# Attribute stage of a graph network kernel: tail repair of two parts moved into the last batches, and twelve row gathers moved ahead of the stage's end

## What is computed

```python
edge_proj = edge_attr @ W_sum + b_sum
sum3d = jax.ops.segment_sum(edge_proj, src, num_segments=num_nodes)
return x + z_in[in_deg] + z_out[out_deg] + cent_term + vor_term + sum3d
```

## Time and profile before

| | us |
|---|---|
| median of 3 runs | 5778.88 |
| lowest and highest | 5772.54, 5779.97 |
| the profiled execution, its own time | 5781.98 |
| its span in the profile | 5780.3 |
| mean granted TensorE clock | 0.711 of full speed |
| busy: PE (TensorE) / DVE / ACT (ScalarE) / POOL | 3737.6 / 4533.3 / 1445.9 / 3515.7 |

### The profile page before, as it was taken

How to read it: one execution, slowest core, us unless ns; L and a number is a source line. 1 busy time by engine, 2 the same in 40 slices (tenths; PEclk the granted TensorE clock), 3 DMA queues, 4 the chain that set the end, 5 groups by cost and what they waited for, 6 DMA issues and landing times.

```text
span 5780.3 us, 46191 instructions
## 1 busy us (share of the span) xinstructions
PE 3737.6 (65%) x13476; PEld 2458.1 (43%) x13476; DVE 4533.3 (78%) x7871; ACT 1445.9 (25%) x4020; POOL 3515.7 (61%) x3626
## 2 busy tenths in 40 slices
PE   2777777986666626999996444444444444455899
PEld 1655666873444415666664111111112111123566
DVE  8787888989356627888766999999999999997334
ACT  1333333333333313333221111111111111112322
POOL 3777777777777775433313777777777777775000
PEclk8555555555555557999998677777777777777899
DMA  3544444444433332211114888888888888886000
GB/s 87 158 157 149 150 152 152 151 146 153 150 103 102 115 108 59 69 59 63 60 40 144 265 287 277 282 282 276 287 277 282 283 277 288 276 277 193 22 20 26
DMA packets 328279, 968.57 MB, mean 168 GB/s; under 512 B 84476, under 2 KB 124101, under 8 KB 315994
## 3 DMA queue, kind: packets, MB, share of 16 engines
q0 software_dynamic: 198672, 578.35, 32.9%
q1 hardware_dynamic: 80970, 211.35, 10.3%
q10 hardware_dynamic: 48384, 175.92, 7.8%
HBM read 670.63 MB, written 294.73 MB: 167 GB/s over the span
## 4 chain that ended last, share of the span: by engine, by line
PE 42%; POOL 28%; issue 11%; ACT 8%; DVE 7%; DMA 2%; ACTq 2%; SPq 0%; DVEq 0%; POOLq 0%
POOL big L1803 25%; PE bank L909 16%; ACT bank L957 6%; PE bank L1556 5%; PE bank L1545 4%; PE bank L855 4%; PE bank L2482 3%; PE bank L2474 3%; POOL big L596 3%; PE bank L1567 2%; ACT big L932 1%; PE bank L2032 1%; ACTq L942 1%; DMA big<-keys_values,idx 1%; PE bank L2357 1%
## 5 line engine op out<-in xcount | busy, mean ns | idle before, releaser
L1803 POOL DMA_INDIRECT big<-keys_values,idx x1674 | 1591.3, 951 | 510.3 <-issue 507.9
L596 POOL DMA_INDIRECT big<-in_edge_attr,big x1568 | 1524.5, 972 | 609.5 <-issue 459.9
L2032 PE MATMUL bank<-big,ident 128*128 128x512 f32 x1674 | 957.3, 738 | 1155.0 <-DVE big L1883 1119.6
L909 PE MATMUL bank<-big,ident 128*128 128x128 f32 x2976 | 1125.0, 481 | 526.6 <-ACT bank L957 508.2
L2032 PEld LDWEIGHTS bank<-big,ident 128*128 128x128 f32 x1674 | 391.8, 241 | 1719.9 <-DVE big L1883 1226.0
L909 PEld LDWEIGHTS bank<-big,ident 128*128 128x128 f32 x2976 | 737.7, 307 | 835.9 <-ACT bank L957 720.9
L957 ACT ACTIVATE bank<-bank,big 128x128 f32<-128x128 f32 x1485 | 508.0, 342 | 1261.8 <-PE bank L909 1256.5
L1905 DVE TENSOR_TENSOR big<-big,bank 128x1536 f32<-128x1536 f32 x279 | 480.0, 1750 | 123.8 <-DMA big<-keys_values,idx 123.8
L648 DVE TENSOR_TENSOR big<-big,bank 128x1024 bf16<-128x1024 bf16 x400 | 486.1, 1215 | 96.8 <-PE bank L855 96.5
L1910 DVE TENSOR_REDUCE big<-big 128x48 f32<-128x1536 f32 x279 | 486.6, 1745 | 0.0
L1915 DVE TENSOR_TENSOR big<-big,bank 128x1536 f32<-128x1536 f32 x279 | 477.9, 1740 | 0.0
(11 more groups left out here) (360 smaller groups left out, 4605.7 us busy)
## 6 DMA issues: line engine op xcount, KB each, us to landing
running_sums<-big ACTq DMA_DIRECT2D x196, 512.0 KB, 2.8
running_attention<-big SPq DMA_DIRECT2D x46, 1632.0 KB, 7.7
queries_by_row<-big ACTq DMA_DIRECT2D x139, 512.0 KB
big<-queries_by_row SPq DMA_DIRECT2D x46, 1536.0 KB, 8.8
big<-keys_values,idx POOLq DMA_INDIRECT x1674, 3.9
big<-in_edge_attr,big POOLq DMA_INDIRECT x1568
keys_values<-big SPq DMA_DIRECT2D x5, 1792.0 KB, 6.9
big<-x_after_layer SPq DMA_DIRECT2D x7, 896.0 KB, 5.6
```

Source lines behind the costliest of these rows:

```text
L596: pool.indirect_dma_start(out=z.rows[:, r, k, :], out_offset=None, in_=w["edge_attr_128"][:, :], in_offset=bass.IndirectOffsetOnAxis(ap=z. ...
L909: pe.matmul(sum_of(k), lhsT=m.ident[:, :], rhs=z.rows[:, r, k, :], start=False, stop=True, skip_group_check=True).then_inc(s_sum, 1)
L1803: pool.indirect_dma_start(out=kv[:, r, k, :], out_offset=None, in_=t["kv"][:, :], in_offset=bass.IndirectOffsetOnAxis(ap=m.idx2[:, c:c + 1 ...
L2032: mm = pe.matmul(bank[pair % 4][:, :], lhsT=m.ident[:, :], rhs=kv[:, b % RINGK, i * S + j:(i + 1) * S + j + 1:S, D:KW], start=(j == 0), st ...
```

## The change

Nothing is computed differently. POOL's list, DVE's tail work and TensorE's tail products are put in another order:

- the three lookups come before the gathers of batch 190, the two row gathers of parts 0 and 1 before batch 192, the two scatters of these parts (each with its wait for landing) before batch 195;
- DVE does `tail_places` for all parts and the additions of parts 0 and 1 after batch 193; only part 2's addition is left behind the last batch;
- the twelve gathers of chunk 0's sums move from the node stage into the attribute stage (`first_sums`, into a buffer of their own, `f.sg0`): eight after the last batch, four after part 2's scatter; four of the eight degree gathers (`z_out`) are now the last thing in POOL's list of the stage;
- the 129 spare rows of `running_sums` move from its end to its beginning, so that gathers from parts 0 and 1 can be declared to read only the rows below part 2;
- POOL, in the node stage, starts with the gathers of chunk 1, after a wait for the twelve.

```diff
-SUMROWS = PLACES + P + 1
+SPARES = P + 1
+SUMROWS = SPARES + PLACES
...
     def gpsimd(pool):
+        def repair(h, q):
+            pool.indirect_dma_start(out=t["sums"][:, :], out_offset=bass.IndirectOffsetOnAxis(ap=q.to_i, axis=0),
+                                    in_=q.main, in_offset=None).then_inc(s_fixed, 16)
+            pool.wait_ge(s_fixed, 16 * (h + 1))
+
+        def first_sums(h):
+            early = slice(0, SPARES + P * PART_START[NP1 - 1]) if h < NP1 - 1 else slice(0, SUMROWS)
+            for b in range(CHUNKS[0]):
+                pool.indirect_dma_start(out=f.sg0[:, h, b, :], out_offset=None, in_=t["sums"][early, :],
+                                        in_offset=bass.IndirectOffsetOnAxis(ap=m.lastpos[:, h, b:b + 1], axis=0)
+                                        ).then_inc(f.rows, 16)
+
         for b in range(B1):
...
+            if b == B1 - 6:
+                pool.wait_ge(s_tabst, 32 * (NP1 + 1))
+                pool.wait_ge(s_trash, 32)
+                for h, q in enumerate(z.tails):
+                    pool.wait_ge(s_look, h + 1)
+                    pool.indirect_dma_start(out=q.row_i, out_offset=None, in_=t["lastpos"][h][:, :],
+                                            in_offset=bass.IndirectOffsetOnAxis(ap=q.look, axis=0)).then_inc(s_found, 16)
+            if b == B1 - 4:
+                pool.wait_ge(s_found, 16 * NP1)
+                for q in z.tails[0:NP1 - 1]:
+                    pool.indirect_dma_start(out=q.main, out_offset=None, in_=t["sums"][0:SPARES + P * PART_START[NP1 - 1], :],
+                                            in_offset=bass.IndirectOffsetOnAxis(ap=q.row_i, axis=0)).then_inc(s_main, 16)
+            if b == B1 - 1:
+                pool.wait_ge(s_fix, NP1 - 1)
+                for h, q in enumerate(z.tails[0:NP1 - 1]):
+                    repair(h, q)
...
-        gather_degrees(pool, m, w, f, 0, range(2, 2 * CHUNKS[0] - NP1))
+        q = z.tails[NP1 - 1]
+        pool.indirect_dma_start(out=q.main, out_offset=None, in_=t["sums"][:, :],
+                                in_offset=bass.IndirectOffsetOnAxis(ap=q.row_i, axis=0)).then_inc(s_main, 16)
+        gather_degrees(pool, m, w, f, 0, range(2, 4))
         pool.wait_ge(s_fix, NP1)
-        for h, q in enumerate(z.tails):
-            pool.indirect_dma_start(out=t["sums"][:, :], out_offset=bass.IndirectOffsetOnAxis(ap=q.to_i, axis=0),
-                                    in_=q.main, in_offset=None).then_inc(s_fixed, 16)
-            gather_degrees(pool, m, w, f, 0, range(2 * CHUNKS[0] - NP1 + h, 2 * CHUNKS[0] - NP1 + h + 1))
-            pool.wait_ge(s_fixed, 16 * (h + 1))
+        repair(NP1 - 1, q)
+        first_sums(NP1 - 1)
+        gather_degrees(pool, m, w, f, 0, range(4, 2 * n))
...
-        for k in range(1, NP1):
-            ins = v.tensor_scalar(z.table[0:64, k], z.table[0:64, k], float(P * PART_START[k]), None, ALU.add)
+        for k in range(NP1):
+            ins = v.tensor_scalar(z.table[0:64, k], z.table[0:64, k], float(SPARES + P * PART_START[k]), None, ALU.add)
...
-        gather(0, 0, NP1 * CB)
-        pool.wait_ge(s_vr, 1)
+        pool.wait_ge(f.rows, 16 * NP1 * CHUNKS[0])
         gather(1, 0, NP1 * CB)
```

More of the change, by code:

```diff
@@ L464, in gpsimd @@
         st.add(pool.iota(m.pidx[:, :], [[0, 1]], base=0, channel_multiplier=1, allow_small_or_imprecise_dtypes=True))
-        st.add(pool.iota(m.trash1[:, :], [[0, 1]], base=PLACES, channel_multiplier=1,
+        st.add(pool.iota(m.trash1[:, :], [[0, 1]], base=0, channel_multiplier=1,
                          allow_small_or_imprecise_dtypes=True))
@@ L472, in gpsimd @@
         st.add(pool.memset(f.nodes, 0.0))
-        st.add(pool.memset(z.trash[:, 0, :], PLACES + P))
+        st.add(pool.memset(z.trash[:, 0, :], P))
         st.add(pool.memset(z.trash[:, 1, :], ROWS + P))
@@ L744, in shadow @@
         for k in range(NP1):
-            st.add(v.tensor_scalar(m.lastpos[:, k, :], last[:, k, :], float(P * PART_START[k]), None, ALU.add))
+            st.add(v.tensor_scalar(m.lastpos[:, k, :], last[:, k, :], float(SPARES + P * PART_START[k]), None, ALU.add))
         st.add(v.tensor_scalar(m.has[:, :], deg, 1.0, None, ALU.min))
@@ L832, in vector @@
                                        in1=z.rows[:, r, k, :], op0=ALU.mult, op1=ALU.add).then_inc(s_sum, 1)
[L833 to L836, removed]
+            if b == B1 - 3:
+                dve.wait_ge(s_found, 16 * NP1)
+                for q in z.tails:
+                    tail_places(dve, v, st, q, m.trash1[:, :])
+                dve.wait_ge(s_prod, 1)
+                dve.wait_ge(s_main, 16 * (NP1 - 1))
+                for h, q in enumerate(z.tails[0:NP1 - 1]):
+                    v.tensor_tensor(q.main, q.main, bank[7][:, h * P:(h + 1) * P], ALU.add).then_inc(s_fix, 1)
+        dve.wait_ge(s_prod, 2)
         dve.wait_ge(s_main, 16 * NP1)
-        for h, q in enumerate(z.tails):
-            v.tensor_tensor(q.main, q.main, bank[7][:, h * P:(h + 1) * P], ALU.add).then_inc(s_fix, 1)
+        q = z.tails[NP1 - 1]
+        v.tensor_tensor(q.main, q.main, bank[7][:, (NP1 - 1) * P:NP1 * P], ALU.add).then_inc(s_fix, 1)
     def tensor(pe):
@@ L916, in tensor @@
         pe.wait_ge(s_eq, 1)
+        pe.wait_ge(s_saved, NP1 - 1)
+        for h, q in enumerate(z.tails[0:NP1 - 1]):
+            mm = pe.matmul(bank[7][:, h * P:(h + 1) * P], lhsT=q.eq, rhs=z.saved[:, h], start=True, stop=True, skip_group_check=True)
+        mm.then_inc(s_prod, 1)
         pe.wait_ge(s_copied, 2 * B1)
[L918 to L922, removed]
+        pe.matmul(bank[7][:, (NP1 - 1) * P:NP1 * P], lhsT=z.tails[NP1 - 1].eq, rhs=z.rows[:, (B1 - 1) % RING1, GB - 1, :],
+                  start=True, stop=True, skip_group_check=True).then_inc(s_prod, 1)
     def scalar(act):
-        into = [t["sums"][P * at:P * (at + n), :].rearrange("(p k) f -> p k f", p=P) for at, n in zip(PART_START, PART_COLS)]
+        into = [t["sums"][SPARES + P * at:SPARES + P * (at + n), :].rearrange("(p k) f -> p k f", p=P) for at, n in zip(PART_START, PART_COLS)]
         qz = t["qrow"][0:ROWS, :].rearrange("(p k) d -> p (k d)", p=P)
@@ L1033, in node_inputs @@
     f.zout, end = cut(m.big, end, CB, D)
+    f.sg0, end = cut(m.big, 4 * CB * D - NP1 * CHUNKS[0] * FE, NP1, CHUNKS[0], FE)
     f.rows = m.sem("node_rows_gathered")
@@ L1123, in node_stage, with sums_of @@
     RA = RV = 4
+    def sums_of(c):
+        return late_sg if c else f.sg0
     def pairs(c, j):
@@ L1197, in gather @@
                 col = slice(CHUNK_AT[c] + b, CHUNK_AT[c] + b + 1)
-                pool.indirect_dma_start(out=sg[:, h, b, :], out_offset=None, in_=t["sums"][:, :],
+                pool.indirect_dma_start(out=late_sg[:, h, b, :], out_offset=None, in_=t["sums"][:, :],
                                         in_offset=bass.IndirectOffsetOnAxis(ap=m.lastpos[:, h, col], axis=0)
```

21 lines of the change are left out of this document (7 added, 14 removed).

## The result

| | before | after |
|---|---|---|
| median (20 runs each) | 5780.51 | 5791.09 |
| lowest and highest | 5772.54, 5785.66 | 5786.03, 5796.85 |
| the profiled execution, its own time | 5781.98 | 5793.27 |
| its span | 5780.3 | 5791.6 |
| mean granted TensorE clock | 0.711 | 0.724 |

Ratio 1.0018, 95% interval 1.0012 to 1.0025: 10.6 us slower, which is inside the 0.2% that I called no change, and not zero. The predicted time was 5786.2 and the range 5779 to 5795.

The account below looks back on a forecast made before the run. POOL's list of DMA issues was taken to bound the attribute stage's end. `mask_sums` 5.3 us late, plus 1.0 for stretched issues and 1.0 for landing under loads, gave 7.3: 5778.88 + 7.3 = 5786.2 us, range 5779 to 5795.

Parts of the forecast that it names:

- the first rival: Node stage opens only when POOL has issued its whole list: `mask_sums` 13.6 us late, 5792.5 us; chance 0.12.
- POOL paces the last batches, each insert is on the path: Last edge batches: inserted lookups, row gathers and scatters add 11.45 us to POOL's list, none of it hidden.
- Hidden inserts: Rival: something other than POOL paces batches 190 to 195, so 11.45 us go: -4.2, 5774.7 us; chance 0.06.
- DVE's part is hidden: After batch 193: DVE's 8.1 us of tail work fit within POOL's 10.3 before the scatters; spare 2.2 us.
- The stage opens at the landing of the third scatter: Node stage's start: DVE begins when that scatter has landed, at 2174.7, 5.95 us late.
- Degree rows become what DVE waits for: Ahead of `add_terms`: DVE waits 1.7 us for the eighth degree gather; `mask_sums` 5.3 us late.
- Stretch of POOL's issues: Degree gathers early in the node stage: POOL's issue takes longer beside DVE's work; 1.0 us, bounds 0 and 1.7.
- Landing under SP's loads: Last degree gathers land in 3.7 us beside SP's loads, 1.0 more than 2.7; bounds 2.7 and 4.6.
- The clock and late stores: TensorE's clock rise: same pattern expected, rival -10 or as much up, chance 0.07; `running_sums` stores: nothing unless over 20 us more.
- the mechanism's own bound: Upper limit of the forecast's lateness with its terms at their bounds: 5.3 + 1.7 + 1.9 + 0.9 = 9.8 us.

Follow-up runs that it names:

- experiment 3: Changed kernel, but POOL leaves the attribute stage only when all eight degree gathers have landed; 5800.73 us, ratio 1.0032 to the kernel before.
- experiment 5: Changed kernel, but the two scatters stand ahead of the first and fourth edge gather of batch 195; 5787.74 us, ratio 1.0009 to the kernel before.
- Experiment 2: Changed kernel, but the last four degree gathers are issued before the four gathers of part 2's sums; 5785.83 us, ratio 1.0005 to the kernel before.
- experiment 4: Changed kernel, but chunk 0's twelve sum gathers return behind the stage's end, degree gathers ahead of the third scatter; 5787.61 us, ratio 1.0007 to before.
- experiment 6: Experiment 4 joined with experiment 5: sums and degree gathers moved back, scatter waits covered; 5780.25 us, ratio 0.9997 to the kernel before.
- experiment 8: Kernel before, but POOL leaves the stage without awaiting the third scatter's landing; its first sum gather waits instead; 5783.36 us, ratio 1.0001.
- experiment 1: Changed kernel, but SP's loads of bias and input rows also wait for the eight degree gathers' landing; 5791.98 us, ratio 1.0014 to before.
- experiment 7: Experiment 6, but POOL leaves the stage once the third scatter is issued; only part 2's sum gathers await its landing; 5778.08 us, ratio 0.9988 to before.

## Why the prediction was right, and what in it was not

The time fell into the range, but that says little about the mechanism. The range was made wide enough for the first rival too, and by the time alone its 5792.5 fits 5791.09 better than my 5786.2 does. What decides is the stage's start in the timeline and experiment 3.

- **POOL paces the last batches, each insert is on the path.** Right. The loop cost 11.73 us (last edge gather, 80.52 for 68.79); predicted 11.45. One of the three scatters landed in 2.7 us, not 2.3, which is the 0.3 that I had left in the bounds. Hidden inserts (-4.2) are ruled out by this and by experiment 5.
- **DVE's part is hidden.** Right: its two additions were done at 2142.56, and POOL came to the scatters at 2144.64 with its usual 0.30 us. The spare was 2.1 us, predicted 2.2.
- **The stage opens at the landing of the third scatter.** Right: L2556 at 2178.81 is 2.3 us behind 2176.49, with eight gathers still to be issued, and experiment 3 shows the 11.7 us of the alternative. Start 6.25 us late; predicted 5.95.
- **Degree rows become what DVE waits for.** Right in kind. Experiment 2 takes the wait away by order alone.
- **Stretch of POOL's issues, predicted 1.0.** Too much: the issues of 2182.79 to 2188.16 took 1.06, 1.06, 1.03, 1.00 and 0.95, together 0.4 us over 0.95 each. What I had not read is where in DVE's work the long issue of before begins. DVE's row of before beside the 1.96 us at 2174.43:

```profile
2174.35 1.23 DVE L1283 TENSOR_TENSOR big<-big 128x1024 f32<-128x1024 f32 x1
```

The issue begins 0.08 us behind this operation. In experiments 3, 4, 6 and 8 one begins 0.08 or 0.09 behind it as well and takes 1.95 or 1.96; in after and in experiments 1, 2 and 5 one begins 0.34 or 0.35 ahead of it and takes 1.06. My own times had an issue at 2179.9 and this operation at 2180.3, so the 1.96 was not to be expected. That it is this operation which stretches the issue is read from the places alone; no run took it away. *By the Trainium skill, "SBUF — State Buffer", "Who interferes with whom", it would be 0: the page has a DVE instruction with two SBUF inputs contend with a GpSimd instruction that reads SBUF, and puts descriptor generation on the writing side, as inferred. The traces don't agree, though after came nearer to 0 than to my 1.0. An indirect gather also takes its row numbers out of a tile (`m.lastpos`), which may put it on the reading side; no run here tells.*
- **Landing under SP's loads, predicted 1.0 more than 2.7.** This is the term that failed. It measured 7.82 us from issue to landing for the gather that counts, 5.1 more than 2.7 and 4.1 more than my term. My upper bound was 4.6, the longest landing of chunk 1's degree gathers; those are issued over 30 us behind the loads, whose longest with a landing in the trace took 9.9 us there (12.4 in after), so they were over and the row bounded nothing here. I had timed the loads' start rightly (6.6 us behind the stage's start, measured 6.65) and then taken the middle between two rows neither of which had a load beside it. *"DMA: Bandwidth & Descriptors" of the Trainium skill, "Issuing engines are not separate DMA queues", named the right mechanism, and the trace agrees with it: 7.3 against 2.9 us with the loads held back.*
- **The clock and late stores.** Nothing came of either, as predicted.

The sum: predicted +7.3 at `mask_sums`, measured +10.9. Of the 3.6 between, 0.3 lies ahead of the stage's start, the rest is the wait in front of `add_terms`: 6.98 us where my terms gave 3.7 (the landing 4.1 more, the stretch 0.6 less, small differences of starts 0.2 less). The 10.9 is 1.1 us beyond the mechanism's own bound of 9.8. In the whole time, 5791.09 is 4.9 above the predicted 5786.2: 3.6 from the sum, 1.6 because the median of before is 5780.51 over twenty runs and was 5778.88 over three, and 0.3 back, since the medians differ by 10.6 and `mask_sums` by 10.9.

Left open: why the loads hold up the gathers by 5 us and not by more or less. Half the loads, or the same bytes in smaller pieces, would tell; neither was tried.

## What to carry to other kernels

Work moved ahead of a wait lets the work behind it start sooner, and that may be the wrong company: here small gathers that DVE waits for were pushed into the first microseconds of large loads, and two lines in the other order get back two thirds of what `mask_sums` had lost. When POOL's issuing is the bound, an edit is worth only the issues and waits that it takes out of POOL's list up to the last row that is needed; a stage opened earlier without that moves a wait and nothing else. Put a scatter where other issues cover its landing: two covered waits gave 3 us.

## What the runs showed of the hardware

- Indirect gathers of 128 rows of 1 KB landed in 2.7 to 3.0 us without the loads (medians of chunk 0's four `z_out`; single degree gathers took up to 3.8) and in 7.3 us (median of four, 7.82 the last) beside 2.8 MB of SP's loads issued within 3 us of them; experiment 5 repeats it with 7.3 and 7.75. The 1 MB load itself took 5.4 there and 5.6 in experiment 5, for 4.5 to 5.1 in the eight kernels in which no degree gather was on its way beside it (4.7 in before): the loads lose little, the gathers much.
- A semaphore addition of POOL was made at 2178.81, while eight indirect DMAs ahead of it in the list were issued only up to 2188.16. It did not pass a wait of its own list for a landing: it came 2.3 us behind the third scatter's start, and in experiment 3, behind a wait for the degree gathers, 11.7 us later.
- POOL's issue of an indirect DMA took 1.95 or 1.96 us for 0.95 where it began 0.08 or 0.09 us behind DVE's operation on 128x1024 (before, experiments 3, 4, 6, 8), 1.35 where it began 0.69 behind (experiment 7), and 1.06 where it began 0.34 or 0.35 ahead (after, experiments 1, 2, 5).
